# The first scan chunk prepared inside the convolution, and each batch's input normalised in an earlier stage

## What is computed

```python
x = x + conv(_gn(x), ...)                 # group norm: 32 groups of 4 channels over the whole image
# inside conv, for each batch:
xz = x @ W_in.T; xc, z = split(xz)        # 128 -> 2 x 256 channels
xc = silu(depthwise_conv3x3(xc) + conv_b)
xs = [rowwise, columnwise, rowwise flipped, columnwise flipped]   # windowed orders of 4096 pixels
dts, Bs, Cs = x_proj(xs); delta = softplus(dt_proj(dts) + bias)
h = exp(delta * A) * h + delta * u * B;  y = sum_n(h * C) + u * D   # 16 states, along 4096 steps
y = layernorm(y) * silu(z);  return y @ W_out.T
```

## Time and profile before

| | us |
|---|---|
| median of 3 runs | 6255.01 (6253.27 to 6257.36) |
| profiled execution, its own time | 6258.71 |
| its span in the trace | 6256.9 |
| PE / PEld busy | 5702.8 (91%) / 5079.1 (81%) |
| DVE / ACT / POOL busy | 4472.1 (71%) / 3169.5 (51%) / 2832.3 (45%) |

### The profile page before, as it was taken

One profiled execution on the slowest core, in us unless ns is written; L12 is line 12 of the kernel. 1 busy time (PEld: TensorE's weight loads), 2 busy tenths in 40 slices (PEclk: granted clock), 3 DMA queues, 4 the chain that ended last, 5 costly groups with the idle time before them and its releaser, 6 DMA issues. The chain is left out here.

```text
span 6256.9 us, 128558 instructions
## 1 busy us (share of the span) xinstructions
PE 5702.8 (91%) x41691; PEld 5079.1 (81%) x41691; DVE 4472.1 (71%) x6306; ACT 3169.5 (51%) x6029; POOL 2832.3 (45%) x1695
## 2 busy tenths in 40 slices
PE   7899999999888999999997659999999899999998
PEld 5688888888667888888885538888888788888887
DVE  2699999999618999999995645555555555555554
ACT  2699888988638998899885221111111111111110
POOL 1699999999608999999994300000000000000000
PEclk8899999999989999999999879999999999999999
DMA  2455555555415555555554147776766666777765
GB/s 96 113 141 144 139 142 143 142 143 137 121 56 136 143 143 139 138 145 145 141 138 124 43 128 156 149 152 147 153 151 149 164 140 151 148 154 149 149 150 143
DMA packets 1098945, 858.32 MB, mean 137 GB/s; under 512 B 305622, under 2 KB 1021238, under 8 KB 1064374
## 3 DMA queue, kind: packets, MB, share of 16 engines
q1 hardware_dynamic: 1097974, 844.72, 55.8%
q10 hardware_dynamic: 720, 10.49, 0.4%
HBM read 811.50 MB, written 43.55 MB: 137 GB/s over the span
## 5 line engine op out<-in xcount | busy, mean ns | idle before, releaser
L726 POOL TENSOR_TENSOR read<-state,c_wide 128x1024 f32<-128x1024 f32 x1024 | 2419.3, 2379 | 213.5 <-DVE state L762 127.3
L762 DVE TENSOR_TENSOR_SCAN state<-decay,carry,p_drive 128x512 f32<-128x512 f32 x1792 | 2140.5, 1258 | 104.0 <-PE p_drive L540 57.2
L658 ACT ACTIVATE decay<-step,a_neg 128x512 f32<-128x512 f32 x2048 | 1398.1, 717 | 223.8 <-DVE state L762 214.3
L1747 PE MATMUL p_y<-window,x_high 128*128 128x256 f32 x7936 | 1495.9, 286 | 0.0
L1811 ACT COPY term_blocks<-p_s 128x256 f32<-128x256 f32 x832 | 310.5, 373 | 2157.2 <-PE p_s L1747 2157.2
L1747 PEld LDWEIGHTS p_y<-window,x_high 128*128 128x128 f32 x7936 | 1243.6, 191 | 0.0
L1747 PE MATMUL p_y<-window,x_low 128*128 128x256 f32 x3968 | 1132.5, 285 | 0.0
L553 PE MATMUL p_y<-ident,read 128*128 128x128 f32 x8192 | 1064.1, 273 | 13.0 <-ACT y_tok L672 3.7
L542 PE MATMUL p_drive<-diag_b,xu_tok 128*128 128x128 f32 x8192 | 1002.7, 276 | 1.3 <-DVE state L762 1.3
L542 PEld LDWEIGHTS p_drive<-diag_b,xu_tok 128*128 128x128 f32 x8192 | 959.2, 193 | 1.6 <-DVE state L762 1.6
L553 PEld LDWEIGHTS p_y<-ident,read 128*128 128x128 f32 x8192 | 925.2, 141 | 25.5 <-issue 21.7
(11 more groups left out here) (257 smaller groups left out, 5443.7 us busy)
## 6 DMA issues: line engine op xcount, KB each, us to landing
c_wide<-c_scratch SPq DMA_DIRECT2D x256, 1024.0 KB, 4.8
window<-taps_scratch SPq DMA_DIRECT2D x576, 257.0 KB, 6.4
diag_b<-diag_scratch SPq DMA_DIRECT2D x256, 512.0 KB, 4.1
window<-taps_scratch SPq DMA_DIRECT2D x768, 129.0 KB, 5.1
window<-taps_scratch SPq DMA_DIRECT2D x128, 513.0 KB, 7.3
window<-taps_scratch SPq DMA_DIRECT2D x64, 385.0 KB, 6.2
gate_scratch<-gate_out SPq DMA_DIRECT2D x16, 512.0 KB, 3.1
gate_in<-gate_scratch SPq DMA_DIRECT2D x8, 1024.0 KB, 6.3
```

Of the source, the lines that this page charges most:

```text
L658: act.activation(decay[:, n % 2, t, :], step[:, c.parity, t, :], ACT.Exp, scale=m.a_neg[:, DT2 * c.k + t, n:n + 1]).then_inc(s["decay"], 1)
L726: pool.tensor_tensor(read[:, n % 4, :, :], state[:, n % 4, :, :], wide, ALU.mult).then_inc(s["read_out"], 1)
L762: dve.tensor_tensor_scan(flip(state[:, n % 4, t, :], c), flip(decay[:, n % 2, t, :], c), flip(p_drive[:, n % 2, t, :], c), 0.0 if c.start ...
L1747: last = pe.matmul(out, x[:, source, blk, :], view[:, :, at:at + P][:, :, ::-1], start=first and x is m.x_high and z == 0, stop=True, skip ...
```

## The change

It does four things.

1. `Image` holds the input's loading, turning and normalising. For batch 0 it runs in `constants`: x is loaded on ACT's queue, turned after the small weights, normalised before `xproj` is filled. For the next batch it runs inside the norm stage of the batch before (after the last batch once more, on batch 0's data, unused). PE turns chunks into the tiles `p_prep` and `p_b`; `x_ch` and `x_tok` are now kept for the whole layer (`x_tok` shares its place with the prepared chunk, `x_ch` with the scan states).
2. `constants` also does the turns of w_z, w_o and w_attn first, stores the conv weights as two halves, waits at its end until they have landed, and `start_counts` runs ahead of it. `convolution` begins with loading the two halves; DVE clears only the borders.
3. The preparation of a batch's first chunk runs between the 16 units of the convolution: `project` after unit 5, `step_product` after 6, `turn_b`, exp and ln after 7, `turn_x` after 11 and 12. The gate tiles lie in the odd chunk's buffers. The loops over g are written out.
4. `begin_y` is cut up: `add_second(g)` does, after each g below 3, the part of it whose pixels are there, in pieces of 64 to 192 elements (columns x rows); g = 3, with 1024 and four times 192 elements a tile, stands at the head of `scans`.

The class and its methods that move data (the small chain keeps its instructions):

```diff
+class Image:
...
+    def load(self, eng):
+        for i in range(4):
+            eng.dma_start(self.m.x_tok[:, 8 * i:8 * i + 8, :], self.x_b[:, 8 * i:8 * i + 8, :]).then_inc(
+                self.s["x_in"][i], 16)
+    def turn(self, pe, c):
+        s, n = self.s, self.n
+        if c % 2 == 0:
+            pe.wait_ge(s["x_in"][c // 2], START + n * 16 + 16)
+        if c >= 2:
+            pe.wait_ge(s["x_ch"], START + n * NCH + (c - 1))
+        for i in range(4):
+            last = pe.transpose(self.pt[c % 2][:, i * P:i * P + P], self.m.x_tok[:, 4 * c + i, :], self.m.ident[:, :])
+        last.then_inc(s["x_t"], 1)
+    def keep(self, act, c):
+        act.wait_ge(self.s["x_t"], START + self.n * NCH + (c + 1))
+        act.copy(self.x_ch[:, c * L:c * L + L], self.pt[c % 2][:, :]).then_inc(self.s["x_ch"], 1)
+    def take_stats(self, dve, c):
+        dve.wait_ge(self.s["x_ch"], START + self.n * NCH + (c + 1))
+        dve.bn_stats(self.stats[:, c, :], self.x_ch[:, c * L:c * L + L]).then_inc(self.s["stats"], 1)
...
+    def centre(self, dve, r):
+        dve.tensor_scalar(self.rows(r), self.rows(r), self.dev[:, 5:6], self.dev[:, 4:5], ALU.subtract,
+                          ALU.mult).then_inc(self.s["centred"], 1)
```

`constants`, in the order SP, ACT, DVE, PE:

```diff
             for parity in range(2):
-                sp.dma_start(m.diag_dram[parity].rearrange("(r x) -> r x", r=P), blank[:, :]).then_inc(m.w_stored, 16)
-            sp.wait_ge(copied, 14)
-            sp.dma_start(m.w_conv_dram, w_conv[:, :, :, :, :].bitcast(fp32).rearrange("p w t a c -> p (w t a c)")
-                         ).then_inc(m.w_stored, 16)
+                sp.dma_start(m.diag_dram[parity].rearrange("(r x) -> r x", r=P), blank[:, :]).then_inc(blanked, 16)
+            sp.wait_ge(copied, 16)
+            for t in range(DT2):
+                sp.dma_start(m.w_conv_dram[t], w_conv[:, :, t, :, :].bitcast(fp32)).then_inc(m.w_stored, 16)
+            sp.wait_ge(blanked, 32)
...
+            image.load(act)
             act.activation(m.a_neg[:, :, :], m.a_neg[:, :, :], ACT.Exp).then_inc(neg_a, 1)
+            for c in range(NCH):
+                image.keep(act, c)
+            image.root(act)
...
+            for c in range(NCH):
+                image.take_stats(dve, c)
+            image.gather(dve)
+            image.deviate(dve)
+            image.keep_variance(dve)
+            image.invert(dve)
+            for r in range(NG):
+                image.centre(dve, r)
             for i in range(NK * DT2):
...
+            pe.wait_ge(copied, 4)
+            for c in range(NCH):
+                image.turn(pe, c)
+            pe.wait_ge(copied, 16)
...
+            image.group_mean(pe)
+            image.group_variance(pe)
```

`convolution` (SP, POOL, PE, ACT, DVE). The methods of `prep` are the functions of `scans` quoted above, unchanged:

```diff
-            x_b = io["x"][ds(b, 1), :, :].rearrange("b (t p) c -> p (b t) c", p=P)
-            for i in range(4):
-                sp.dma_start(x_tok[:, 8 * i:8 * i + 8, :], x_b[:, 8 * i:8 * i + 8, :]).then_inc(s["x_in"][i], 16)
-            sp.wait_ge(m.w_stored, 48)
-            sp.dma_start(w_conv[:, :, :, :, :].bitcast(fp32).rearrange("p w t a c -> p (w t a c)"),
-                         m.w_conv_dram).then_inc(s["w_in"], 16)
-            with sp.Fori(0, NG) as g:
+            for t in range(DT2):
+                sp.dma_start(w_conv[:, :, t, :, :].bitcast(fp32), m.w_conv_dram[t]).then_inc(s["w_in"][t], 16)
...
+                if g == 1:
+                    prep.store_rows(sp, nc, chunk)
...
+                                       ALU.mult).then_inc(m.sem_b["y_begun"], 1)
+                if g == 1:
+                    prep.step_times_u(pool, chunk)
...
-            with pe.Fori(0, NG) as g:
+            for g in range(NG):
...
+                        if g == 0 and half == 0:
+                            pe.wait_ge(s["w_in"][t], START + b * 16 + 16)
...
+                        unit = 4 * g + 2 * half + t
+                        if unit == 5:
+                            pe.wait_ge(s["gated"], START + b * 17 + 5)
+                            prep.project(pe, chunk)
+                        if unit == 6:
+                            prep.step_product(pe, chunk, 0)
+                            prep.step_product(pe, chunk, 1)
+                        if unit == 7:
+                            prep.turn_b(pe, chunk)
+                        if unit in (11, 12):
+                            prep.turn_x(pe, chunk, unit - 11)
...
-            act.wait_ge(s["gn"], START + b * 5 + 4)
-            act.activation(dev[:, 3:4], dev[:, 2:3], ACT.Sqrt, bias=m.eps[:, 0:1]).then_inc(s["gn_sqrt"], 1)
             act.sem_inc(s["gated"], 1)
+            act.wait_ge(s["padded"], START + b * 4 + 4)
             for r in range(NG):
-                act.wait_ge(s["centred"], START + b * NG + (r + 1))
                 act.copy(inner(high, r), rows(r)).then_inc(s["high"], 1)
-            with act.Fori(0, NG) as g:
+            for g in range(NG):
...
+                        unit = 4 * g + 2 * half + t
+                        if unit == 5:
+                            prep.keep_projection(act, chunk)
+                        if unit == 6:
+                            prep.step_parts(act, chunk)
+                        if unit == 7:
+                            prep.keep_b(act, chunk)
+                            act.preload_act_table_set("natural_log_exp_and_others")
+                            prep.step_exp(act, chunk)
+                            prep.step_ln(act, chunk)
+                        if unit in (11, 12):
+                            prep.keep_x(act, chunk, unit - 11)
...
-            dve.memset(high[:, :, :].bitcast(fp32), 0.0).then_inc(s["padded"], 1)
-            dve.memset(low[:, :, :].bitcast(fp32), 0.0).then_inc(s["padded"], 1)
+            for image in (high, low):
+                rim = image[:, :, :].bitcast(fp32)
+                dve.memset(rim[:, ::H + 1, :], 0.0).then_inc(s["padded"], 1)
+                dve.memset(rim[:, 1:1 + H, ::W + 1], 0.0).then_inc(s["padded"], 1)
...
+            for g in range(NG - 1):
+                for t in range(DT2):
+                    dve.wait_ge(s["gated"], START + b * 17 + g * 4 + (4 + t))
+                    dve.wait_ge(m.sem_b["y_begun"], START + b * 8 + (2 * g + t + 1))
+                    add_second(dve, m, g, t)
+                if g == 1:
+                    prep.finish_step(dve, chunk)
```

The pieces of the second product, and the head of the DVE list in `scans`:

```diff
+def add_second(dve, m, g, t):
+    y = m.y[:, t, :].rearrange("p (h w) -> p w h", w=W)
+    x = m.s2[:, t, :].rearrange("p (w h) -> p w h", h=H)
+    new, past = slice(WIN * g, WIN * (g + 1)), slice(0, WIN * g)
+    last = g == NCH // 2 - 1
+    pieces = [(slice(0, W), new)] if last else []
+    for w in range(0, W, WIN):
+        pieces.append((slice(w + 4 * g, w + 4 * g + 4), past if last else slice(0, WIN * (g + 1))))
+        if g and not last:
+            pieces.append((slice(w, w + 4 * g), new))
+    for columns, rows in pieces:
+        ins = dve.scalar_tensor_tensor(y[:, columns, rows], x[:, columns, rows], m.d_skip[:, 10 + t:11 + t],
+                                       y[:, columns, rows], ALU.mult, ALU.add)
+    return ins
...
-                    begin_y(0)
-                    finish_step(c)
-                    begin_y(1)
+                    for t in range(DT2):
+                        add_second(dve, m, 3, t).then_inc(s["y_whole"], 1)
```

`norm_and_project` (SP, PE, ACT, DVE; k is the iteration):

```diff
+            image.load(sp)
...
+                if k in (3, 4, 5, 6):
+                    image.turn(pe, 2 * k - 6)
+                    image.turn(pe, 2 * k - 5)
+                if k == 7:
+                    image.group_mean(pe)
+                if k == 8:
+                    image.group_variance(pe)
...
+                if k in (3, 4, 5, 6):
+                    image.keep(act, 2 * k - 6)
+                    image.keep(act, 2 * k - 5)
+            image.root(act)
...
+                if k in (3, 4, 5, 6):
+                    image.take_stats(dve, 2 * k - 6)
+                    image.take_stats(dve, 2 * k - 5)
+                if k == 6:
+                    image.gather(dve)
+                if k == 7:
+                    image.deviate(dve)
+                if k == 8:
+                    image.keep_variance(dve)
+                if k == 9:
+                    image.invert(dve)
+                    image.centre(dve, 0)
+                    image.centre(dve, 1)
+                if k == 10:
+                    image.centre(dve, 2)
+                    image.centre(dve, 3)
```

`program`:

```diff
+            ready = sb0("chunk_ready", [P, XD + 2 * NB4 * NS + 10 * L])
+            m.x_tok = ready[:, 0:T // P * C].rearrange("p (t c) -> p t c", c=C)
...
+            m.gate = [m.step[:, 1], m.xu_tok[:, 1].rearrange("p (t i) d -> p t (i d)", t=DT2)]
+            m.p_prep = layer0.enter_context(nc.psum_tensor("p_prep", [P, L], fp32))
+            m.p_b = layer0.enter_context(nc.psum_tensor("p_b", [P, L], fp32))
+            m.x_ch = sb0("x_ch", [P, T])
```

More of the change, by code:

```diff
@@ L193, in _ @@
             last.then_inc(multiplied, 1)
-            pe.wait_ge(copied, 14)
+            for t in range(DT2):
```

(17 more changed lines are left out.)

421 lines of the change are left out of this document (209 added, 212 removed).

## The result

| us | before | changed |
|---|---|---|
| median of 20 runs each, same chip | 6258.74 | 6244.76 |
| ratio, 95% interval | | 0.9979 [0.9972, 0.9985] |
| span of the profiled execution | 6256.9 | 6238.5 |

The change saves 14 us, just past the 12.5 that the prediction called distinguishable. The forecast was 6214.5 and its range ended at 6240: the sign is right, the size is not, and the time lies outside the range.

The account below looks back on a forecast made before the run. PE bounds the convolution; at the head of the scans the first chunk's preparation is late. Terms -47.2 + 12.0 - 33.6 + 8.0 + 20.3 = -40.5 took the profiled 6258.7 to 6218.2, or 6214.5 for the median; range 6193 to 6240.

Parts of the forecast that it names:

- leaves the long loops alone: Whole kernel: the change touches only the seams between stages; the scans' own chunks got no term in the sum.
- Rival (c): Convolution written out: PE's longer list makes each matmul 0.06 us later, 58 us lost, 6272; chance 0.04.
- if the scans' own chunks change: Scans: one of the signs named as proving the forecast wrong.
- Head of the scans: Start of the scans: preparation leaves, first scan 8.7 us after block start instead of 32.3; -47.2 us in all.
- Convolution: Convolution's units: PE, the bound there, gets 6.0 us more work a batch; +12.0 us.
- (b): Seams: DVE's pieces at twice the rate per element, POOL held back, weights' half late; 25 us less gained, 6239; chance 0.12.
- (d): Convolution: preparation holds PE up as `turn_x` waits for POOL, 7 us a batch, 6229; chance 0.08.
- Head of the convolution: Convolution's start: first matmul 6.7 us after block start, on the weights' first half, instead of 23.2 and 23.8; -33.6 us.
- Constants: Constants stage: 10.4 us of work added on DVE, less 2.4 beside waits; +8.0 us net, bounds +3 and +15.
- Norm stage: Norm stage: copies and statistics lengthen the ring by 2.8 us in four iterations; +20.3 us for both batches, bounds 8 and 30.
- Rival (a): Norm stage: its DMA waits absorb the longer ring, only about 4 us a batch appear; 6202, chance 0.14.

Follow-up runs that it names:

- pad30_after: Changed kernel with 30 one-column memsets on VectorE in the convolution, where it is idle: 6219.84 us against 6259.0 for the kernel before, ratio 0.9941.
- x_behind: Changed kernel with x's four loads issued by SyncE behind the small loads, none by ScalarE: 6236.83 us against 6259.0 for the kernel before, ratio 0.9963.
- ring: Changed kernel; norm stage's ScalarE copies moved in front of `affine`, VectorE's statistics behind the next `centre`: 6233.53 us against 6261.69 before, ratio 0.9954.
- 49: Changed kernel with 49 one-column memsets on VectorE in the convolution, where it is idle: 6240.23 us in a single run.
- late_x: Changed kernel with ScalarE issuing x's four loads only after the small loads have landed: 6251.08 us against 6261.69 for the kernel before, ratio 0.9984.
- long_before: Kernel before with 36 satisfied semaphore waits per chunk on VectorE, 18 of them becoming instructions: 6280.47 us in a single run, against 6266.94.

## Why the prediction was wrong

**The step that failed** is its first sentence on the kernel, that the change "leaves the long loops alone": the scans' own chunks stood in the sum at nothing, without a row. It leaves their body alone and moves it in VectorE's list by 48 instructions, and that cost 19.2 us in the scans (21.4 by the spans of changed kernel and pad30_after, two kernels that differ in 30 idle memsets alone). Rival (c) did ask after the supply of instructions, but on PE, where code became straight; there nothing happened, a conv unit without extra work takes 7.16 us by the starts of ScalarE's reads, 7.16 on average before too. The prediction named "if the scans' own chunks change" as what would prove it wrong, and that is how it went. With the loops on clean places and all else as in the change, the chip gives 6219.84, 39 less than before: 5 us from the forecast, inside its range, and with some help of chance: the errors of the other terms, -2.0 to +4.3 us, add up to 2.9 only. Of the 30.3 us between forecast and median, 22.1 are the terms of the table; 3.7 the forecast had taken off because its three runs had a median of 6255.01 (twenty runs gave 6258.74, the time of the profiled execution itself), and 4.6 is how far the changed kernel's profiled execution lay below its median.

**Head of the scans**: right. Ten pieces in 8.49 us, 8.4 by the sum. By the fixed latency in the Trainium skill ("VectorE: DVE Perf Modes", the TRN2 errata) it would have been 9.1, an estimate; the row was the better guide: the pieces of 192 elements last 0.62 to 0.67 us each, but start only 0.54 apart. **Convolution**: right, +10.0 for +12.0; five units longer by 0.4 to 2.1 us, the two with `project` and `step_product` most. Rivals (b) and (d) did not occur. **Head of the convolution**: right, 5.7 and 6.3 us for 6.7, and the weights' DMA releases it.

**Constants**: mis-sized twice, with opposite signs. That the 2 MB of x delay the small weights, in the prediction a bound, was the true case for 6.7 us and belonged into the sum; against it, all else that the stage was given costs 4.7 (41.1 in x_behind against 36.40), not 8.0. VectorE's first instruction behind the loads before, then in the changed kernel, and its last of the stage there:
```profile
10.68 0.23 DVE L129 TENSOR_SCALAR a_neg<-a_neg 128x128 f32<-128x128 f32 x1 [8.63 <-ACT a_neg L120]
```
```profile
21.63 0.23 DVE L220 TENSOR_SCALAR a_neg<-a_neg 128x128 f32<-128x128 f32 x1 [15.49 <-ACT a_neg L208]
...
47.01 1.27 DVE L234 COPY w_dt<-wps 8x512 f32<-8x512 f32 x2
```
From there to its end VectorE's list takes 26.7 us instead of 20.7 (31.4 less 10.68): of the 10.4 us of added work 4.5 lay beside waits, not 2.4.

**Norm stage**: right in mechanism and size (period 8.05 for 8.1 forecast, +22.1 for +20.3). Rival (a) did not occur. (The "56 us" that the prediction gives the stage is its window up to 1712; the stage lasts 63.8 us. No term hangs on it.) What the forecast took as given, the place of the copies in the ring, was a choice: ring gets 15.5 of the 22.1 back.

The range failed above all for one reason: its bounds held every term that I had a row for, and nothing for code that moves.

## What to carry to other kernels

An edit that adds instructions ahead of a hardware loop can slow that loop by microseconds a jump, with no change in it and no engine to blame: compare the packets of the instruction queues (q14 here) with those of the kernel before, and if they rose, shift the loop by a few dozen idle instructions and count again. A shift can also make a clean loop stall, as 49 did for the third direction. When work is moved into a ring of two engines, look where each idles in its iteration and put it there, not behind the last instruction. When a DMA issue is moved, read what stands behind it on the issuing engine, and what else the queues carry at that time.

## What the runs showed of the hardware that was not expected

Stalls of 0.9 to 5.7 us at VectorE's jump back in a loop of 280 instructions that begins at 41 to 61 of 128 (36 and 64 are clean), with 5 more packets of 8.2 KB on an instruction queue for each. Why one such jump costs 0.9 us and another 5.7 stays open; it was not tried. Four issues of 512 KB loads took 3.88 us on SyncE's queue (x_behind), 5.57 on ScalarE's beside small loads (changed kernel), and 12.31 there beside 4 MB of stores (late_x), and the engine's activations wait for that long. And the gap that such a stall leaves can carry another engine's name (5.51 us "POOL carry" in long_before, where VectorE stood from 349.3 to 354.84).
